# Two steps of a graph-network kernel put elsewhere: a head's 32x32 block turn into the slot that makes it, and a piece of a product ahead of a transposition

## What is computed

```python
for l in range(3):                                    # first network
    si = x @ attn_w[l, :d]; sj = x @ attn_w[l, d:]
    scores = leaky_relu(si[:, :, None] + sj[:, None, :] + attn_b[l], 0.2)
    attn = softmax(where(mask, scores, -inf))
    h = layernorm(x + attn @ x, g1[l], beta1[l])
    x = layernorm(h + gelu(h @ W1[l] + b1[l]) @ W2[l] + b2[l], g2[l], beta2[l])
x1 = layernorm(x0 + x)
xh = heads(x1 @ W_proj)                               # second network, 8 heads
att = softmax(where(mask, leaky_relu(a_src + a_dst + b_att, 0.2), -1e30))
out = layernorm(x1 + relu(att @ xh))
```

## Time and profile before

| | |
|---|---|
| median of 3 runs | 2283.65 us (2283.08 to 2285.51) |
| the profiled execution | 2286.04 us, its span 2284.3 us |
| TensorE (PE) busy | 2180.6 us, 95% |
| VectorE (DVE) busy | 1851.9 us, 81% |
| ScalarE (ACT) busy | 1643.8 us, 72% |
| chain that ended last | PE 77%, DVE 15%, ACT 4% |
| mean granted TensorE clock | 0.984 |

### The profile page before, as it was taken

One profiled execution on the slowest core, in us unless ns is written; L12 is line 12 of the kernel. 1 busy time (PEld: TensorE's weight loads), 2 busy tenths in 40 slices (PEclk: granted clock), 3 DMA queues, 4 the chain that ended last, 5 costly groups with the idle time before them and its releaser, 6 DMA issues.

```text
span 2284.3 us, 31680 instructions
## 1 busy us (share of the span) xinstructions
PE 2180.6 (95%) x10181; PEld 1529.3 (67%) x10181; DVE 1851.9 (81%) x5742; ACT 1643.8 (72%) x3163; POOL 198.5 (9%) x200
## 2 busy tenths in 40 slices
PE   5999999999999999999999999999999999999966
PEld 3766767667776776677667667766766777677543
DVE  5565788889788888878798897888888888988777
ACT  2434468777778777886787777787778777887786
POOL 0010110010100110001100101001010010001100
PEclk9999999999999999999999999999999999999977
DMA  6011026443174243551354431743326423453111
GB/s 224 10 37 37 28 97 191 131 135 121 47 223 147 74 139 91 182 153 65 125 168 142 139 117 50 224 141 97 125 79 208 130 69 107 132 154 116 38 43 37
DMA packets 130273, 261.22 MB, mean 114 GB/s; under 512 B 9368, under 2 KB 58812, under 8 KB 122172
## 3 DMA queue, kind: packets, MB, share of 16 engines
q1 hardware_dynamic: 130108, 259.19, 36.4%
HBM read 185.49 MB, written 73.66 MB: 113 GB/s over the span
## 4 chain that ended last, share of the span: by engine, by line
PE 77%; DVE 15%; ACT 4%; issue 2%; POOL 2%; DMA 0%; DVEq 0%; POOLq 0%; ACTq 0%
PE ffn L1261 23%; PE av L1178 14%; PE ffn L1250 11%; PE av L1250 11%; PE pT L1161 7%; PE av L1202 5%; PE av L1237 2%; DVE prob L793 2%; DVE prob L784 2%; ACT xs L568 1%; DVE stats L732 1%; POOL rstd L485 1%; PE trow L1140 1%; DVE xs L919 1%; DVE xs L913 1%
## 5 line engine op out<-in xcount | busy, mean ns | idle before, releaser
L1261 PE MATMUL ffn<-w_sb,G 128*128 128x256 f32 x3072 | 734.8, 381 | 0.0
L1261 PEld LDWEIGHTS ffn<-w_sb,G 128*128 128x128 f32 x3072 | 565.8, 191 | 99.0 <-issue 29.3
L793 DVE CUSTOM_DVE_ANT_0 prob<-trow,mask 128x512 f32<-128x512 f32 x676 | 438.8, 685 | 28.2 <-PE trow L1140 15.2
L1250 PE MATMUL ffn<-hT,w_sb 128*128 128x512 f32 x768 | 355.0, 595 | 0.9 <-issue 0.9
L1250 PE MATMUL av<-hT,w_sb 128*128 128x512 f32 x768 | 354.0, 593 | 0.0
L485 POOL TENSOR_TENSOR rstd<-veps,mhalf 128x4 f32<-128x4 f32 x127 | 167.3, 1317 | 2047.8 <-DVE veps L728 2047.8
L528 ACT ACTIVATE prob<-prob,s 128x512 f32<-128x512 f32 x484 | 331.5, 716 | 3.9 <-DVE nm L800 3.9
L534 ACT ACTIVATE prob<-prob,nm 128x512 f32<-128x512 f32 x448 | 317.7, 712 | 0.0
L1161 PEld LDWEIGHTS pT<-ident,prob 128*128 128x128 f32 x1712 | 216.7, 144 | 128.0 <-issue 87.1
L1161 PE MATMUL pT<-ident,prob 128*128 128x128 f32 x1712 | 264.4, 279 | 21.3 <-DVE prob L856 9.3
L1178 PE MATMUL av<-xs,prob 128*128 128x257 f32 x1024 | 244.2, 380 | 9.0 <-DVE prob L863 9.0
(11 more groups left out here) (154 smaller groups left out, 2742.8 us busy)
## 6 DMA issues: line engine op xcount, KB each, us to landing
blocks_dram<-blocks SPq DMA_DIRECT2D x248, 256.0 KB, 4.2
prob<-blocks_dram SPq DMA_DIRECT2D x62, 1024.0 KB, 4.8
w_sb<-in_L_gnn_W SPq DMA_DIRECT2D x48, 1024.0 KB, 8.9
trow<-rows_dram SPq DMA_DIRECT2D x127, 256.0 KB, 3.2
adj_sb<-in_adj SPq DMA_DIRECT2D x16, 1024.0 KB, 5.6
xin<-in_x SPq DMA_DIRECT2D x16, 512.0 KB, 6.4
x0r<-in_x SPq DMA_DIRECT2D x16, 512.0 KB, 5.8
out<-o SPq DMA_DIRECT2D x15, 512.0 KB, 2.9
```

The lines of the kernel that those rows point to most:

```text
L793: return v.tensor_tensor_reduce(out=out_[:, t, :], in0=targets, in1=mask[:, t, :], scale=1.0, scalar=LEAST, op0=ALU.add, op1=ALU.max, accu ...
L1250: last = te.matmul(ff1[f % len(ff1)][:], w1_sb[:, g // 2 % STAGES, dt, f * P:(f + 1) * P], hT[:, dt, :], start=dt == 0, stop=dt == DT - 1)
L1261: last = te.matmul(ffn[part][:, at:at + D], G[:, f, t * P:(t + 1) * P], w2_sb[:, g // 2 % STAGES, f, :], start=f == 0, stop=f == FT - 1)
```

## The change

Head 0 of a pair is turned in slot 0, the one that makes its exponentials, as VectorE's last work ahead of the second half of `fed_forward`, and no longer in slot 1 ahead of the attention. SP's `move` of it goes along. Heads 1 and 2 stay where they are, as slot 1 leaves `AHEAD` and both were behind the attention already. In slot 4 (`place == 2`) the four pieces of the second loop go 1, 2, 0, 1 in place of 1, 1, 1, 1.

```diff
-AHEAD = (1, 2, 3, 4)
+AHEAD = (2, 3, 4)
+
+SOON = (0,)
...
+def turned_soon(g):
+
+    return [q for q in made(g)[:1] if moved(q) and q % (2 * HEADS) in SOON]
+
+
+def turned_later(g):
+    return [q for q in turned(g) if moved(q) and q % (2 * HEADS) not in SOON]
+
+
 def turned_ahead(g):
-    return [q for q in turned(g) if moved(q)][:1] if g % SLOTS in AHEAD else []
+    return turned_later(g)[:1] if g % SLOTS in AHEAD else []
 
 
 def turned_behind(g):
 
-    return [q for q in turned(g) if moved(q)][len(turned_ahead(g)):]
+    return turned_later(g)[len(turned_ahead(g)):]
...
-                for q in turned_behind(g)[1:]:
+                for q in turned_behind(g)[1:] + turned_soon(g):
                     move(q)
...
-                for q in turned_behind(g)[1:]:
+                for q in turned_behind(g)[1:] + turned_soon(g):
                     turn_blocks(q)
                 fed_forward(s, 1)
...
-                    pieces(1)
+
+                    pieces((1, 2, 0, 1)[t] if place == 2 else 1)
```

## The result

The change takes 2271.62 us, the median of six runs (2269.86 to 2272.94); the kernel before takes 2283.54 us in the six runs beside them. The ratio is 0.9945, with a 95% interval of 0.9932 to 0.9958: 11.9 us faster, where 10.0 were forecast. Direction and places were right, and the size was short by a sixth.

The account below looks back on a forecast made before the run. TensorE, 95% busy, was taken as the bound, its waits as the target. 9.0 us (slot 1) plus 1.0 (slot 4) made 10.0 off the 2283.65 median: 2273.6 us; range 2271.7 to 2278.1.

Parts of the forecast that it names:

- Part 1, the wait goes in full: Slot 1: moving head 0's turn out removes TensorE's whole wait for VectorE's attention reading, 9.0 us in six slots.
- Slack of the first reading: Slot 1: without the turn VectorE's first attention reading ends at 620.22, 0.92 us before TensorE's third product wants it.
- The turn in slot 0 costs nothing: End of slot 0: the 2.31 us turn fits VectorE's 7.02 us wait and leaves 4.7; cost nothing.
- SP and the transfers at nothing: Slot 0: SP's move, issued at about 592, delays nothing queued; the same 2 MB cross earlier; cost nothing.
- Second pair gives nothing: Slot 1 of the second pair: TensorE did not wait there, so the seventh moved turn gains nothing.
- Part 2: Slot 4: moved piece fills TensorE's wait ahead of the transposition; 0 to 0.26 us a slot, 0.15 taken, 1.0 us.
- The new wait in front of L1202: Slot 4, ahead of the heads' product: TensorE would newly wait some 0.7 us for ScalarE's copies.
- the expected wait of 0.1: Slot 5: a TensorE wait of about 0.1 us in front of the attention's first product.
- A: Slot 1: another wait takes the place of the 1.47 us one, half of 9.0 gained; 2278.1 us; chance 10%.
- B: Slot 0: the moved turn is not covered by idle time and slot 1's wait returns; 2282.6 us; chance 6%.
- C: Slot 4: the moved piece gives nothing or all; 2274.6 or 2272.9 us, inside the forecast's range; no separate chance.
- D: Slot 4: TensorE's clock drops to 1.2 GHz over 16 unbroken transposes, +12.5 us; 2287.2 us; chance 4%.

Follow-up runs that it names:

- the filler: Against the change: a VectorE write of 128x1024 zeros to the emptied blocks buffer added in slot 1 ahead of the attention; 2274.46 us in one run.

## Why the prediction was off, step by step

- **Part 1, the wait goes in full: right, its size wrong.** The failed step is "PE was free for it at 622.61 - 1.47 = 621.14", and with it "9.0 us in six slots". A printed end lies 0.16 behind the point at which the next matmul begins when nothing waits, and the bracket counts from that printed end. The earlier trace rows show both: the turn starts at 620.54, its successor would follow 0.43 or 0.44 later, so TensorE stood from 620.98 and not 621.14. The wait was 1.63, the restart cost 0.07, and 1.70 by six slots is 10.2. The seventh pair's longer wait adds 0.24, which the brackets' 9.0 held too, and the fifth pair's 0.31 makes it 10.8, though that went with VectorE's pause and isn't shown to be of the change. By these numbers the sum is 10.8 + 1.2 = 12.0, and 2283.54 - 12.0 = 2271.5; measured 2271.62. That it fits to 0.1 is partly luck: what stands behind the last slot counted took between 163.3 and 166.1 us in the ten profiles, 165.6 before and 166.1 in the change.
- **Slack of the first reading.** By the same step it is less than the 0.92 I gave. The reading ends at 618.41 in the change and the product begins at 619.14, 0.73 later, and some of that is the way from one engine to the other (0.15 before: the reading ends at 622.46, the product begins at 622.61). Enough, and by the filler it was 0.59.
- **The turn in slot 0 costs nothing: right.** 4.78 us of cover are left (4.7 forecast), and without cover the gain is gone.
- **SP and the transfers at nothing: right.** The move is issued at 590.00, and slots 2 and 3 are unchanged.
- **Second pair gives nothing: right.** 42.63 before, 42.64 after.
- **Part 2: right in sum, and in mechanism but for one term.** Expected at 0.15 a pair within 0 to 0.26, measured 0.37 - 0.20 = 0.17. Slot 4 alone gained more than the 0.2 to 0.3 named. The copies end 0.24 earlier in the slot, as forecast with 0.26, but "the product started 0.18 after the copy" was no delay of the copy's: TensorE was still at its piece. In the change, where it does wait, the product starts 0.05 after the copy. The new wait in front of L1202 was to be 0.7; its bracket shows 0.42, and start to start it is 764.65 - 763.20 - 0.87 = 0.58. In slot 5 the expected wait of 0.1 appears in no bracket at all, only as 0.20 of length: a wait shorter than the overlap is not shown. The 0.1 for the signal had no row; where an engine waits, the rows here show 0.05 to 0.15.
- **The rivals.** A (another wait in slot 1) did not come. B's condition never held; made to hold, it took 2284.8 where the price was 2282.6, and the waits stood elsewhere. C did not come either: part 2 gave 0.17 a pair, neither nothing nor all. D did not come: in the unbroken run of transposes the granted clock was 1.00, the 2.4 GHz level, so nothing of D is borne out:

```profile
761.00:764.60 3.60, 3.00 (x21) 2.38 (x20) 2.66 (x9) 3.60 (x8) 1.92 (x1) 1.00 0.00 0
```

- **The range.** It put 1.2 us for the spread of the runs under an upper bound of part 2, and nothing for the size of part 1, the largest term, as I took the bracket for a measurement. With 0.2 us a wait either way, 1.2 in all, it would have held the time.

## What to carry to other kernels

In every wait read here, a bracket of idle time in front of a pipelined matmul was a lower bound of what the wait cost: take the start-to-start distance and subtract the one of the same neighbours where nothing waits. Waits below the overlap show no bracket; compare the lengths of stages instead. And before a step is hurried on the busiest engine, ask whose chain reaches the next stage just as late: here 0.37 gained in one slot gave back 0.20 in the next, and a further 0.55 gave back all, until VectorE's work was moved out of that chain.

## What the runs showed of the hardware that was not expected

**The price of a TensorE wait.** Bracket plus 0.16 us (four transposes print 0.60 and are followed after 0.44) plus a restart, 0.07 or 0.08 where eight products of the attention follow (they last 1.98 and not 1.91), 0.05 and 0.11 elsewhere. Brackets of 0.27, 0.75 and 1.47 cost 0.51, 1.01 and 1.70, and those of 1.07 and 0.51 in one slot together 2.06.

**POOL beside VectorE.** The shift of 128x4 took 1.27 us where it began within 0.01 us of VectorE's 1.22 us sum of two tensors (L1000), and 0.20 where that sum was made to wait. The Trainium skill, SBUF — State Buffer, SBUF: two separate sides, says that a VectorE operation with two SBUF inputs and a GpSimd operation that reads SBUF hold one port pair by turns, each for its whole length. The two rows agree with it: the slow shift ended 0.06 us behind the sum (759.24 and 759.18). Not starting beside the sum is worth 1.07 us to the shift; no run here lets the shift begin just ahead of a sum that does not wait.

**A dip of the clock that moves.** Each of the ten profiles has one slot among the first seven that is 1.69 us longer than in others: the second pair's slot 0 in some, the first pair's slot 4 in the rest. In the two below the clock was granted 0.66 on average over 5 us there, so for a part at the 1.2 GHz level. Before, at the end of the second pair's slot 0:

```profile
324.20:329.20 5.00, 5.00 (x18) 4.11 (x17) 0.39 (x4) 5.00 (x10) 0.00 (x0) 0.66 0.15 52
```

and in the change at the end of the first pair's slot 4:

```profile
240.10:245.10 5.00, 5.00 (x18) 4.07 (x17) 1.68 (x14) 2.54 (x3) 0.00 (x0) 0.66 0.48 133
```

Sixteen products took 5.31 us there and 3.62 elsewhere, 1.69 each time, so it cancels between the two. In both they follow a transposition that had waited, 1.97 us before and 2.46 in the change, but such a wait does not bring the dip each time: in the kernel before, the first pair's slot 4 has one of 2.47 and no dip. The program's start does not cancel: the second slot begins at 84.72 before and at 83.03 in the change, in a region where the clock still rises from its 1.2 GHz level (mean 0.58 granted from 42 to 49 us before, 0.74 in the change). The two profiled spans differ by 13.1 us, of which this is 1.7, and behind the last slot counted the change is 0.5 longer; the medians differ by 11.9. What sets the place of the dip no run here tells.
